# A GRU scan step: the scan's addends move from SBUF to PSUM, and the copy that feeds them moves from VectorE to ScalarE

## The chip, the core and the metric

The kernel runs on one core of a Trainium2 chip. The metric is device time in microseconds (us) of one execution. Engines are named as in the profile: PE (TensorE matmuls), PEld (TensorE weight loads), DVE (VectorE), ACT (ScalarE), POOL, SP. SBUF and PSUM are the core's two on-chip memories; matmuls write PSUM.

## The reference

Eight sequences of 256 steps with 256 channels go through a modulated linear layer and then a GRU, each with a residual:

```
ys = cond / 16;  d = rsqrt((ys*ys) @ (w*w) + 1e-8)
x  = x + ((x * ys) @ w) * d
for t in 0..255:
    Z = sigmoid(Xz[t] + H @ Whz.T + bhz)
    R = sigmoid(Xr[t] + H @ Whr.T + bhr)
    N = tanh(Xh[t] + (R*H) @ Whh.T + bhh)
    H = Z*H + (1 - Z)*N
    Y[t] = H @ Whq.T + bhq
x  = x + Y
```

Xz, Xr, Xh are x @ Wx.T + bx. The time goes into the 256 dependent steps.

## The kernel before

Channels lie on the 128 partitions in two chunks (k = 0, 1), so that one step's state is 2 x 8 columns. Time is cut into 16 blocks (n) of 16 steps (j). float32 is kept by splitting a factor into three bf16 parts; a product of weights and state is then six bf16 matmuls (3 x part 0, 2 x part 1, 1 x part 2), so that one gate of one step takes 24 small matmuls of 8 columns.

Each engine's program is written out by hand in its own order, and semaphores join them. One step t is:

- PE: 24 matmuls of gate R (they wait for `h_ready`, then `h_rest`, `h_rest2`), 12 of gate Z with 24 columns, one "bulk" matmul, 24 of gate G (these wait for `rh_ready`), five more bulk matmuls of 128 columns. Bulk is the work on other blocks, spread over the steps: for j < 4 the output Y of the block before, into `y_bank`, for j = 4 to 7 gate Z of the next block, into `z_bank`, for j >= 8 gates R and G of the next block, into `chunk_bank`. In 16 steps (n = 0 with j >= 4, n = 1 with j < 4) the bulk is one float32 matmul instead. Some steps have none (n = 0 with j < 4, n = 15 with j = 4 to 7).
- ACT: two sigmoids of R (L325, PSUM to PSUM), the sigmoid of -Z that writes 1 - Z into `scan_mul` (L327), two Tanh of the candidate N (L330), the copy that seeds gate Z's bank for the next step (L305), and in four steps of a block a copy that seeds a gate's bank (L311).
- DVE: R*H (L517) and its two remainders (L521, L525), a reduce that sums Z's partial products (L529), in most steps one 128-column instruction of the block work (L489 `finish`, L396 `take_z`, L413 `add_x`, L402, L409), two scans (L563), the remainders of the new H (L357, L361), and two copies (L364, L365).

The update of H is a scan over 24 columns, three for each sequence. It runs state = mul * state + add, with mul = 0, -1, 1-Z and add = h, N, h. That leaves h, then N - h, then (1-Z)(N-h) + h in the three columns, and the third is the new H. In `hidden[:, k, slot, 0:24]` the scan leaves its output; the addends lie in the same tensor, from column 2 of the slot before: h is in columns 2, 5, ... (the previous scan left it there), Tanh writes columns 3, 6, ..., and the copy L365 writes h once more to columns 4, 7, .... The scan waits for `g_ready`, which Tanh raises.

`r_gate` chooses the bank in which the R gate of a step lies: `r_bank` for k = 0, and for k = 1 `z_bank` while bulk works in `y_bank` (n > 0, j < 4), else `y_bank`.

Of the kernel before, what the change touches and what calls it, by code (L numbers as in the profile page):

```python
# [5 lines left out]
def modulated_linear_then_gru(  # L6
# [37 lines left out]
    ALU = mybir.AluOpType  # L44
    ACT = mybir.ActivationFunctionType

    P = 128
    KC = x_cm.shape[1]
    C = P * KC
    B = cond_cm.shape[2]  # L50
    T = x_cm.shape[2] // B
    BLOCK = 16
    BC = BLOCK * B
    SLOTS = 2 * BLOCK
# [11 lines left out]
    with ctx:  # L66
        def sb(name, shape, dt=fp32):
            return ctx.enter_context(nc.sbuf_tensor(name, shape, dt))
# [45 lines left out]


        PART = 3 * B
        hidden = sb("hidden", [P, KC, SLOTS, 2 * PART])
        hidden_parts = sb("hidden_parts", [P, KC, SLOTS, PARTS, B])
        r_hidden = sb("r_hidden", [P, KC, PARTS, B])
        z_pre = sb("z_pre", [P, KC, B])  # L120
# [14 lines left out]
        def h_scanned(k, slot):  # L135
            return hidden[:, k, slot, 2:PART:3]
# [19 lines left out]
        y_bank = pb("y_bank")  # L156
        r_bank = pb("r_bank")

        def r_gate(k, n, j):

            bank = r_bank if k == 0 else (z_bank if n > 0 and j < 4 else y_bank)
            return bank[:, KC * BC:KC * BC + B]

        def lin_bank(i, m):

# [2 lines left out]
        def pre(parity, gate, m, lo, hi):  # L168

            if gate == Z:  # L170
                return z_bank[:, m * BC + lo * B:m * BC + hi * B]
            at = 0 if gate == R else BC
            return chunk_bank[parity][m][:, at + lo * B:at + hi * B]
# [112 lines left out]
        @block.scalar  # L286
        def _(act):
            act.dma_start(cond[:, :, :], cond_cm).then_inc(ld_cond, 16)
            act.dma_start(w_mod[:, :, :], w_mod_cm).then_inc(ld_wmod, 16)
            act.dma_start(bias_rows[:, :, :], gate_bias[0:2, :, :]).then_inc(ld_bias, 16)  # L290
            act.dma_start(z_bx_bh[:, :, :], z_bias).then_inc(ld_zbias, 16)
            act.dma_start(bq[:, :], out_bias).then_inc(ld_bq, 16)

            act.wait_ge(ones_ready, 1)
            nc.scalar.activation(table_warm[:, :], ones[:, :], ACT.Sigmoid)
            act.wait_ge(ld_wrec, 16)
            for gate in GATE_ORDER:
                nc.scalar.activation(w_part[0][:, gate, :, :], w_rec[:, gate, :, :], ACT.Copy).then_inc(part_ready, 1)
            for i, gate in enumerate(GATE_ORDER):
                act.wait_ge(rest_ready, i + 1)  # L300
                nc.scalar.activation(w_part[1][:, gate, :, :], w_rec_rest[:, gate, :, :], ACT.Copy).then_inc(part_ready, 1)

            def seed_z(parity, j):

                nc.scalar.activation(  # L305
                    z_rec_bank[:, 0:KC * Z_GROUPS * B].rearrange("p (m g b) -> p m g b", m=KC, g=Z_GROUPS)[:, :, PARTS, :],
                    z_in[:, parity, :, j, :], ACT.Copy).then_inc(z_seeded, 1)

            def seed_gate(parity, gate, k):

                nc.scalar.activation(chunk_bank[parity][k][:, gate * BC:(gate + 1) * BC], bias_wide[:, k, gate, :],  # L311
                                     ACT.Copy).then_inc(gates_seeded, 1)

            act.wait_ge(wide_ready, 1)
            act.wait_ge(lin_ready, 1)
            for i in range(2 * KC):
                seed_gate(0, i // KC, i % KC)
            act.wait_ge(z_seeded, 1)
            act.wait_ge(lin_ready, 3)

            for t in range(T):
                p, j, n = t // BLOCK % 2, t % BLOCK, t // BLOCK
                for k in range(KC):
                    act.wait_ge(pre_r[k], t + 1)
                    nc.scalar.activation(r_gate(k, n, j), pre(p, R, k, j, j + 1), ACT.Sigmoid).then_inc(r_ready[k], 1)  # L325
                act.wait_ge(pre_z, t + 1)
                nc.scalar.activation(scan_mul[:, :, 2::3], z_pre[:, :, :], ACT.Sigmoid, scale=-1.0)  # L327
                for k in range(KC):
                    act.wait_ge(pre_g[k], t + 1)
                    nc.scalar.activation(hidden[:, k, (t - 1) % SLOTS, 3:3 + PART:3], pre(p, G, k, j, j + 1),  # L330
                                         ACT.Tanh).then_inc(g_ready[k], 1)
                if t + 1 < T:
                    seed_z((t + 1) // BLOCK % 2, (t + 1) % BLOCK)
                if n + 1 < NB and j in (4, 5, 6, 7):
                    if j == 4:
                        act.wait_ge(lin_ready, GROUPS)
                    seed_gate(1 - p, (j - 4) // KC, j % KC)

        @block.vector
        def _(dve):  # L340
# [8 lines left out]
            def split_h(slot, t1):  # L349
# [12 lines left out]
                                            ).then_inc(h_rest2[k], 1)  # L362
                if t1 <= T:
                    nc.vector.tensor_copy(h_word(every_chunk, slot), h_scanned(every_chunk, slot)).then_inc(h_packed, 1)  # L364
                nc.vector.tensor_copy(hidden[:, :, slot, 4:4 + PART:3], h_scanned(every_chunk, slot))  # L365

            nc.vector.memset(zeros[:, :], 0.0).then_inc(zeros_ready, 1)
            dve.wait_ge(ld_cond, 16)
# [135 lines left out]
            for t in range(T):  # L504
# [9 lines left out]
                    weight_split(6 + j % 2, 1 + (j - 4) // 2)  # L514
                for k in range(KC):
                    dve.wait_ge(r_ready[k], t + 1)
                    nc.vector.tensor_tensor(r_hidden[:, k, 0, :], r_gate(k, n, j), h_scanned(k, before),  # L517
                                            ALU.mult).then_inc(rh_ready[k], 1)
                for k in range(KC):
                    dve.wait_ge(rh_ready[k], t + 1)  # L520
# [2 lines left out]
                for k in range(KC):  # L523
# [6 lines left out]
                    z_pre[:, :, :], z_rec_bank[:, 0:KC * Z_GROUPS * B].rearrange(  # L530
                        "p (m g b) -> p m b g", m=KC, g=Z_GROUPS),
                    axis=mybir.AxisListType.X, op=ALU.add).then_inc(pre_z, 1)
                if n > 0 and j in (4, 5):
                    finish(n - 1, j - 4)
                if n + 1 < NB and j in (8, 9):
                    if j == 8:
                        dve.wait_ge(z_ready, n + 1)
                    take_z(1 - p, j - 8)
                if n == LAST and j in (14, 15):
                    finish_last(0, j - 14)  # L540
                if n == 0 and j < 4:
# [4 lines left out]
                    if j == 3:  # L546
                        mul.then_inc(lin_ready, 1)
                if NB // GROUPS <= n + 2 < NB:
                    if j == 10:
                        dve.wait_ge(lin_ready, GROUPS)  # L550
                    if j in (10, 11):
                        add_x(j - 10, slice((n + 2) * BC, (n + 3) * BC)).then_inc(x1_ready, 1)
                if n + 2 < NB:
                    if j in (12, 13):
                        if j == 12:
                            dve.wait_ge(x1_ready, x1_count(n + 2))
                        first_x1_rest(n + 2, j - 12)
                    if j in (14, 15):
                        second_x1_rest(n + 2, j - 14)

                for k in range(KC):
                    dve.wait_ge(g_ready[k], t + 1)
                    nc.vector.tensor_tensor_scan(hidden[:, k, t % SLOTS, 0:PART], scan_mul[:, k, :],  # L563
                                                 hidden[:, k, before, 2:2 + PART], 0.0, ALU.mult, ALU.add
                                                 ).then_inc(h_ready[k], 1)
                split_h(t % SLOTS, t + 2)

# [259 lines left out]
```

## Time and profile before

| | us |
|---|---|
| median of three runs | 640.48 (639.31 to 640.96) |
| the profiled execution | 639.56 |
| its span in the profile | 637.8 |
| lowest to highest of the three, share | 0.26% |

Busy shares of the span are 98% for PE, 89% for PEld, 77% for DVE and 33% for ACT. A busy share says little here: matmuls are pipelined and their ends are modelled, so that PE is shown as busy while the next matmul waits for its input. What a step waits for is read from the timeline of a step: where an instruction starts a few hundredths of a microsecond after another engine's instruction ended, that one released it.

### The profile page before, as it was taken

To read this page: it belongs to the slowest core of one execution; us is meant where nothing else is said; L and a number is where in the kernel's file an instruction comes from. 1 tells how busy PE (TensorE), PEld (TensorE's weight loads), DVE (VectorE), ACT (ScalarE), POOL (GpSimd) and SP (SyncE) were. 2 spreads that over 40 slices of the span, in tenths; PEclk is the share of its full clock that TensorE was granted. 3 is DMA by queue.
4 is the path that set the end of the run, shared out by engine and by line. 5 is a ranking of instruction groups with operands and counts; after the bars stand their busy time and mean duration, and the time that the engine had idled before them with its cause. 6 is when DMAs were issued, how large, how long until landed. Compare 5 with 4: busy or idle time off the path is not lost.

```text
span 637.8 us, 39807 instructions
## 1 busy us (share of the span) xinstructions
PE 626.3 (98%) x16890; PEld 568.1 (89%) x16890; DVE 491.6 (77%) x4051; ACT 209.1 (33%) x1607; POOL 4.5 (1%) x11
## 2 busy tenths in 40 slices
PE   8999999999999999999999999999999999999987
PEld 3689999999999999999999999999999999999976
DVE  5789777777877778777877877777777777877776
ACT  3133333333233333333333333333333333333332
POOL 2000000000000000000000000000000000000000
PEclk9955555555555555555555555555555555555555
DMA  7000000000000000000000000000000000000000
GB/s 264 2 5 3 4 13 4 13 4 12 4 5 12 5 12 4 12 5 4 13 4 13 4 5 12 5 12 5 12 5 4 12 4 13 4 13 4 4 12 12
DMA packets 7174, 8.86 MB, mean 14 GB/s; under 512 B 1618, under 2 KB 5458, under 8 KB 6996
## 3 DMA queue, kind: packets, MB, share of 16 engines
q1 hardware_dynamic: 6416, 6.03, 2.9%
q8 instruction: 133, 2.18, 1.4%
q14 instruction: 45, 0.37, 0.2%
q10 hardware_dynamic: 580, 0.28, 0.2%
HBM read 4.21 MB, written 2.10 MB: 10 GB/s over the span
## 4 chain that ended last, share of the span: by engine, by line
PE 93%; DVE 4%; ACT 1%; DMA 1%; issue 1%; DVEq 0%
PE chunk_bank L670 53%; PE z_rec_bank L670 13%; PE chunk_bank L647 12%; PE y_bank L632 6%; PE z_bank L647 6%; PE chunk_bank L679 1%; DMA x<-x_cm 1%; PE chunk_bank L584 1%; DVE lin L383 1%; DVE r_hidden L517 1%; DVE hidden L563 1%; DVE r_hidden L521 0%; DVE r_hidden L525 0%; ACT scan_mul L327 0%; DVE xs L376 0%
## 5 line engine op out<-in xcount | busy, mean ns | idle before, releaser
L670 PE MATMUL chunk_bank<-r_hidden,w_part 128*128 128x8 bf16 x6144 | 206.2, 169 | 0.2
L670 PEld LDWEIGHTS chunk_bank<-r_hidden,w_part 128*128 128x128 bf16 x6144 | 184.7, 105 | 17.9 <-issue 0.6
L670 PEld LDWEIGHTS chunk_bank<-hidden,w_part 128*128 128x128 bf16 x3072 | 102.5, 104 | 34.5 <-DVE hidden L563 6.2
L670 PE MATMUL chunk_bank<-hidden,w_part 128*128 128x8 bf16 x3072 | 125.1, 173 | 4.5 <-DVE hidden L563 4.0
L563 DVE TENSOR_TENSOR_SCAN hidden<-scan_mul,hidden 128x24 f32<-128x24 f32 x512 | 80.7, 199 | 60.0 <-ACT hidden L330 53.8
L327 ACT ACTIVATE scan_mul<-z_pre 128x16 f32<-128x16 f32 x256 | 57.2, 223 | 197.1 <-DVE z_pre L529 197.1
L670 PE MATMUL z_rec_bank<-hidden_parts,w_part 128*128 128x24 bf16 x3072 | 121.5, 181 | 0.1
L670 PE MATMUL chunk_bank<-hidden_parts,w_part 128*128 128x8 bf16 x3072 | 119.3, 168 | 0.0
L325 ACT ACTIVATE r_bank<-chunk_bank 128x8 f32<-128x8 f32 x256 | 41.5, 162 | 212.1 <-PE chunk_bank L670 206.6
L670 PEld LDWEIGHTS z_rec_bank<-hidden_parts,w_part 128*128 128x128 bf16 x3072 | 103.2, 104 | 0.2 <-DVE z_rec_bank L465 0.2
L670 PEld LDWEIGHTS chunk_bank<-hidden_parts,w_part 128*128 128x128 bf16 x3072 | 102.9, 104 | 0.0
L517 DVE TENSOR_TENSOR r_hidden<-r_bank,hidden 128x8 f32<-128x8 f32 x256 | 42.7, 167 | 73.4 <-ACT r_bank L325 73.2
L330 ACT ACTIVATE hidden<-chunk_bank 128x8 f32<-128x8 f32 x512 | 72.3, 179 | 3.1 <-PE chunk_bank L670 3.1
L357 DVE TENSOR_TENSOR hidden_parts<-hidden 128x8 f32<-128x8 f32 x514 | 71.3, 170 | 0.0
L361 DVE TENSOR_TENSOR hidden_parts<-hidden_parts 128x8 f32<-128x8 f32 x514 | 70.5, 167 | 0.0
L525 DVE TENSOR_TENSOR r_hidden<-r_hidden 128x8 f32<-128x8 f32 x512 | 70.3, 167 | 0.0
L521 DVE TENSOR_TENSOR r_hidden<-r_hidden 128x8 f32<-128x8 f32 x512 | 70.2, 167 | 0.0
L647 PE MATMUL chunk_bank<-x_rest,w_in 128*128 128x128 bf16 x224 | 58.4, 308 | 0.0
L529 DVE TENSOR_REDUCE z_pre<-z_rec_bank 128x16 f32<-128x64 f32 x256 | 55.7, 217 | 0.0
L305 ACT ACTIVATE z_rec_bank<-z_in 128x16 f32<-128x16 f32 x255 | 47.2, 185 | 0.0
L365 DVE COPY hidden<-hidden 128x16 f32<-128x16 f32 x257 | 44.5, 173 | 0.0
L632 PE MATMUL y_bank<-hidden_parts,w_out 128*128 128x128 bf16 x168 | 44.2, 295 | 0.0
(86 smaller groups left out, 667.3 us busy)
## 6 DMA issues: line engine op xcount, KB each, us to landing
x<-x_cm SPq DMA_DIRECT2D x4, 512.0 KB, 7.9
out_cm<-result SPq DMA_DIRECT2D x15, 128.0 KB, 2.1
w_rec<-w_rec_cm SPq DMA_DIRECT2D x1, 768.0 KB, 8.2
w_in<-w_in_cm SPq DMA_DIRECT2D x1, 768.0 KB, 9.8
w_mod<-w_mod_cm ACTq DMA_DIRECT2D x1, 256.0 KB, 5.7
w_out<-w_out_cm SPq DMA_DIRECT2D x1, 256.0 KB, 10.3
out_cm<-result SPq DMA_DIRECT2D x1, 64.0 KB, 2.9
out_cm<-result SPq DMA_DIRECT2D x2, 32.0 KB, 1.9
```

Source lines behind the costliest of these rows:

```text
L327: nc.scalar.activation(scan_mul[:, :, 2::3], z_pre[:, :, :], ACT.Sigmoid, scale=-1.0)
L330: nc.scalar.activation(hidden[:, k, (t - 1) % SLOTS, 3:3 + PART:3], pre(p, G, k, j, j + 1), ACT.Tanh).then_inc(g_ready[k], 1)
L357: nc.vector.tensor_tensor(h_word(k, slot, 1), h_scanned(k, slot), h_scanned_high(k, slot), ALU.subtract).then_inc(h_rest[k], 1)
L361: nc.vector.tensor_tensor(h_word(k, slot, 2), h_word(k, slot, 1), h_parts(k, slot, 1, 2), ALU.subtract).then_inc(h_rest2[k], 1)
L517: nc.vector.tensor_tensor(r_hidden[:, k, 0, :], r_gate(k, n, j), h_scanned(k, before), ALU.mult).then_inc(rh_ready[k], 1)
L521: nc.vector.tensor_tensor(r_hidden[:, k, 1, :], r_hidden[:, k, 0, :], rh_parts(k, 0, 1), ALU.subtract).then_inc(rh_rest[k], 1)
L525: nc.vector.tensor_tensor(r_hidden[:, k, 2, :], r_hidden[:, k, 1, :], rh_parts(k, 1, 2), ALU.subtract).then_inc(rh_rest2[k], 1)
L529: nc.vector.tensor_reduce(z_pre[:, :, :], z_rec_bank[:, 0:KC * Z_GROUPS * B].rearrange("p (m g b) -> p m b g", m=KC, g=Z_GROUPS), axis=myb ...
L563: nc.vector.tensor_tensor_scan(hidden[:, k, t % SLOTS, 0:PART], scan_mul[:, k, :], hidden[:, k, before, 2:2 + PART], 0.0, ALU.mult, ALU.ad ...
L632: mm = nc.tensor.matmul(y_bank[:, m * BC:(m + 1) * BC], W_OUT[wp][:, k, cols], h_parts(k, slice((1 - p) * BLOCK, (2 - p) * BLOCK), part, p ...
L647: mm = nc.tensor.matmul(pre(1 - p, gate, m, 0, BLOCK), W_IN[wp][:, gate, k, cols], x1_part(n + 1, k, part), start=(j == 4 and i == 0), sto ...
L670: return nc.tensor.matmul(cols, w_part[wp][:, gate, k, m * P:(m + 1) * P], moving, start=first, stop=True, skip_group_check=True)
```

## The change

Tanh now writes PSUM, into a stretch of 24 columns behind the R gate in the same bank, and the scan reads its 24 addends there. The two h columns of each three, which were there already (column 2) or were written by DVE (L365), are now both written by two ACT copies, `feed_scan`, one for each chunk. They wait for `h_ready` and stand behind the copy that seeds gate Z. DVE's copy L365 is gone, and `hidden` has half its width. The bank for k = 1 is chosen by `step_bank` so that bulk never works in it during the step; it is `z_bank` also for j = 8 and 9; `finish`, which reads `y_bank`, moves from j = 4, 5 to j = 8, 9, `take_z` from 8, 9 to 12, 13, `add_x` from 10, 11 to 4, 5, the first remainder of x from 12, 13 to 10, 11. Two waits are new on ACT, at the places where the copies for the next step would enter a bank in which bulk still works.

```diff
-        hidden = sb("hidden", [P, KC, SLOTS, 2 * PART])
+        hidden = sb("hidden", [P, KC, SLOTS, PART])
...
-        def r_gate(k, n, j):
-
-            bank = r_bank if k == 0 else (z_bank if n > 0 and j < 4 else y_bank)
-            return bank[:, KC * BC:KC * BC + B]
+        def step_bank(k, t):
+
+            n, j = t // BLOCK, t % BLOCK
+            return r_bank if k == 0 else (z_bank if n > 0 and (j < 4 or j in (8, 9)) else y_bank)
+
+        def r_gate(k, t):
+
+            return step_bank(k, t)[:, KC * BC:KC * BC + B]
+
+        def scan_add(k, t):
+
+            return step_bank(k, t)[:, KC * BC + 2 * B:KC * BC + 2 * B + PART]
...
+            def feed_scan(t):
+
+                for k in range(KC):
+                    act.wait_ge(h_ready[k], t + 1)
+                    nc.scalar.activation(scan_add(k, t).rearrange("p (b i) -> p b i", i=3)[:, :, 0::2],
+                                         h_scanned(k, (t - 1) % SLOTS).unsqueeze(2).to_broadcast([P, B, 2]), ACT.Copy)
...
-                    nc.scalar.activation(hidden[:, k, (t - 1) % SLOTS, 3:3 + PART:3], pre(p, G, k, j, j + 1),
+                    nc.scalar.activation(scan_add(k, t)[:, 1::3], pre(p, G, k, j, j + 1),
                                          ACT.Tanh).then_inc(g_ready[k], 1)
...
+                if t + 1 < T:
+                    if n > 0 and j == 3:
+                        act.wait_ge(y_ready, n)
+                    if 0 < n < NB - 1 and j == 7:
+                        act.wait_ge(z_ready, n + 1)
+                    feed_scan(t + 1)
...
-                nc.vector.tensor_copy(hidden[:, :, slot, 4:4 + PART:3], h_scanned(every_chunk, slot))
...
-                if n > 0 and j in (4, 5):
-                    finish(n - 1, j - 4)
+                if n > 0 and j in (8, 9):
+                    finish(n - 1, j - 8)
...
                     nc.vector.tensor_tensor_scan(hidden[:, k, t % SLOTS, 0:PART], scan_mul[:, k, :],
-                                                 hidden[:, k, before, 2:2 + PART], 0.0, ALU.mult, ALU.add
+                                                 scan_add(k, t), 0.0, ALU.mult, ALU.add
                                                  ).then_inc(h_ready[k], 1)
```

On ACT, an ordinary step in the middle of a block, from the sigmoid of Z to the next R sigmoids, stood before as

```order
L327 ACTIVATE scan_mul<-z_pre 128x16 [waits pre_z]
L330 ACTIVATE hidden<-chunk_bank 128x8 [waits pre_g0]
L330 ACTIVATE hidden<-chunk_bank 128x8 [waits pre_g1]
L305 ACTIVATE z_rec_bank<-z_in 128x2x8
L325 ACTIVATE r_bank<-chunk_bank 128x8 [waits pre_r0]
L325 ACTIVATE y_bank<-chunk_bank 128x8 [waits pre_r1]
```

and now stands, at the end of step j = 3, where the wait for bulk's last matmul in `y_bank` is added, as

```order
L343 ACTIVATE scan_mul<-z_pre 128x16 [waits pre_z]
L346 ACTIVATE r_bank<-chunk_bank 128x8 [waits pre_g0]
L346 ACTIVATE z_bank<-chunk_bank 128x8 [waits pre_g1]
L313 ACTIVATE z_rec_bank<-z_in 128x2x8
L326 ACTIVATE r_bank<-hidden 128x8x2 [waits h_ready0,y_ready]
L326 ACTIVATE y_bank<-hidden 128x8x2 [waits h_ready1]
L341 ACTIVATE r_bank<-chunk_bank 128x8 [waits pre_r0]
L341 ACTIVATE y_bank<-chunk_bank 128x8 [waits pre_r1]
```

Tanh's destination changed, and the two copies L326 came between the seed of gate Z and the R sigmoids of the next step.

On DVE, the end of step j = 4 of a block and the start of the next, with the block work in front of the scans, stood before as

```order
L529 TENSOR_REDUCE z_pre<-z_rec_bank 128x16 [waits rec_z]
L489 SCALAR_TENSOR_TENSOR result<-y_bank,bq,x 128x128 [waits stored1,y_ready]
L563 SCALAR_TENSOR_TENSOR hidden<-scan_mul,hidden 128x24 [waits g_ready0]
L563 SCALAR_TENSOR_TENSOR hidden<-scan_mul,hidden 128x24 [waits g_ready1]
L357 TENSOR_TENSOR hidden_parts<-hidden 128x8 [waits h_ready0]
L357 TENSOR_TENSOR hidden_parts<-hidden 128x8 [waits h_ready1]
L361 TENSOR_TENSOR hidden_parts<-hidden_parts 128x8 [waits h_rest0]
L361 TENSOR_TENSOR hidden_parts<-hidden_parts 128x8 [waits h_rest1]
L364 COPY hidden_parts<-hidden 128x2x8
L365 COPY hidden<-hidden 128x2x8
L517 TENSOR_TENSOR r_hidden<-r_bank,hidden 128x8 [waits r_ready0]
```

and the place where `finish` stands now, step j = 8, reads

```order
L550 TENSOR_REDUCE z_pre<-z_rec_bank 128x16 [waits rec_z]
L510 SCALAR_TENSOR_TENSOR result<-y_bank,bq,x 128x128 [waits stored1,y_ready]
L584 SCALAR_TENSOR_TENSOR hidden<-scan_mul,r_bank 128x24 [waits g_ready0]
L584 SCALAR_TENSOR_TENSOR hidden<-scan_mul,z_bank 128x24 [waits g_ready1]
L379 TENSOR_TENSOR hidden_parts<-hidden 128x8 [waits h_ready0]
L379 TENSOR_TENSOR hidden_parts<-hidden 128x8 [waits h_ready1]
L383 TENSOR_TENSOR hidden_parts<-hidden_parts 128x8 [waits h_rest0]
L383 TENSOR_TENSOR hidden_parts<-hidden_parts 128x8 [waits h_rest1]
L386 COPY hidden_parts<-hidden 128x2x8
L538 TENSOR_TENSOR r_hidden<-r_bank,hidden 128x8 [waits r_ready0]
```

The scans (shown as SCALAR_TENSOR_TENSOR) now have a PSUM bank as their second input, and the copy behind L364 is gone. PE's order is unchanged.

## Rows read from the trace of the kernel before

**Rows 1.** The page: granted clock of 40 slices, and the final chain by engine.
```profile
PEclk9955555555555555555555555555555555555555
...
PE 93%; DVE 4%; ACT 1%; DMA 1%; issue 1%; DVEq 0%
```

**Rows 2.** Three stretches of four steps: busy us (count) by engine, clock, DMA.
```profile
308.52:318.01 9.49, 9.49 (x267) 8.75 (x266) 7.53 (x63) 3.39 (x28) 0.00 (x0) 0.50 0.02 4
607.31:616.79 9.48, 7.99 (x246) 7.38 (x246) 7.06 (x62) 2.99 (x26) 0.00 (x0) 0.50 0.07 18
56.86:66.49 9.63, 9.57 (x249) 8.91 (x249) 8.38 (x67) 3.00 (x26) 0.00 (x0) 0.50 0.02 4
```

**Rows 3.** Timeline of one step's end: start, us, engine, line, instruction, count [idle before].
```profile
308.19 0.22 ACT L327 ACTIVATE scan_mul<-z_pre 128x16 f32<-128x16 f32 x1 [0.77 <-DVE z_pre L529]
...
308.31 0.29 ACT L330 ACTIVATE hidden<-chunk_bank 128x8 f32<-128x8 f32 x2
...
308.51 0.31 PE L647 MATMUL z_bank<-x_rest,w_in_rest 128*128 128x128 bf16 x1
...
308.52 0.32 DVE L563 TENSOR_TENSOR_SCAN hidden<-scan_mul,hidden 128x24 f32<-128x24 f32 x2 [0.36 <-ACT hidden L330]
...
308.59 0.27 ACT L311 ACTIVATE chunk_bank<-bias_wide 128x128 f32<-128x128 f32 x1
308.62 0.31 PE L647 MATMUL z_bank<-x_rest,w_in 128*128 128x128 bf16 x1
...
308.78 0.15 PEld L670 LDWEIGHTS chunk_bank<-hidden,w_part 128*128 128x128 bf16 x3
308.79 0.22 PE L670 MATMUL chunk_bank<-hidden,w_part 128*128 128x8 bf16 x2
```

**Rows 4.** The same timeline, a step without bulk.
```profile
607.57 0.49 PE L670 MATMUL chunk_bank<-hidden,w_part 128*128 128x8 bf16 x12 [0.41 <-DVE hidden L563]
```

**Rows 5.** ACT's instructions by line and shape: busy us, mean ns of one | idle before.
```profile
L330 ACT ACTIVATE hidden<-chunk_bank 128x8 f32<-128x8 f32 x512 | 72.3, 179 | 3.1 <-PE chunk_bank L670 3.1
L327 ACT ACTIVATE scan_mul<-z_pre 128x16 f32<-128x16 f32 x256 | 57.2, 223 | 197.1 <-DVE z_pre L529 197.1
L305 ACT ACTIVATE z_rec_bank<-z_in 128x16 f32<-128x16 f32 x255 | 47.2, 185 | 0.0
...
L325 ACT ACTIVATE y_bank<-chunk_bank 128x8 f32<-128x8 f32 x196 | 31.7, 162 | 0.0
```

**Rows 6.** DVE's instructions by line and shape.
```profile
L563 DVE TENSOR_TENSOR_SCAN hidden<-scan_mul,hidden 128x24 f32<-128x24 f32 x512 | 80.7, 199 | 60.0 <-ACT hidden L330 53.8
...
L521 DVE TENSOR_TENSOR r_hidden<-r_hidden 128x8 f32<-128x8 f32 x512 | 70.2, 167 | 0.0
...
L517 DVE TENSOR_TENSOR r_hidden<-y_bank,hidden 128x8 f32<-128x8 f32 x196 | 32.7, 167 | 0.0
...
L465 DVE TENSOR_SCALAR z_rec_bank<-z_bank,bias_z 128x8 f32<-128x8 f32 x2 | 0.4, 228 | 0.0
...
L440 DVE TENSOR_SCALAR d_sq<-z_rec_bank 128x16 f32<-128x16 f32 x1 | 0.2, 174 | 0.3 <-PE z_rec_bank L577 0.3
```

**Rows 7.** Timeline of DVE ahead of the steps.
```profile
18.81 1.28 DVE L383 TENSOR_TENSOR lin<-chunk_bank,d 128x512 f32<-128x512 f32 x2
20.01 1.28 DVE L376 TENSOR_TENSOR xs<-x,ys 128x512 f32<-128x512 f32 x2
```

**Rows 8.** Timeline of ACT, then of DVE, after the scans of Rows 3.
```profile
309.53 0.16 ACT L325 ACTIVATE r_bank<-chunk_bank 128x8 f32<-128x8 f32 x1 [0.66 <-PE chunk_bank L670]
...
309.24 0.17 DVE L365 COPY hidden<-hidden 128x16 f32<-128x16 f32 x1
309.72 0.17 DVE L517 TENSOR_TENSOR r_hidden<-r_bank,hidden 128x8 f32<-128x8 f32 x1 [0.30 <-ACT r_bank L325]
```

**Rows 9.** Timeline of DVE around a `finish`, step j = 4.
```profile
265.37 0.34 DVE L489 SCALAR_TENSOR_TENSOR result<-y_bank,bq,x 128x128 f32<-128x128 f32 x1
265.82 0.32 DVE L563 TENSOR_TENSOR_SCAN hidden<-scan_mul,hidden 128x24 f32<-128x24 f32 x2
```

More of the change, by code:

```diff
@@ L319, in _ @@
             act.wait_ge(lin_ready, 3)
+            feed_scan(0)
             for t in range(T):
@@ L324, in _ @@
                     act.wait_ge(pre_r[k], t + 1)
-                    nc.scalar.activation(r_gate(k, n, j), pre(p, R, k, j, j + 1), ACT.Sigmoid).then_inc(r_ready[k], 1)
+                    nc.scalar.activation(r_gate(k, t), pre(p, R, k, j, j + 1), ACT.Sigmoid).then_inc(r_ready[k], 1)
                 act.wait_ge(pre_z, t + 1)
@@ L516, in _ @@
                     dve.wait_ge(r_ready[k], t + 1)
-                    nc.vector.tensor_tensor(r_hidden[:, k, 0, :], r_gate(k, n, j), h_scanned(k, before),
+                    nc.vector.tensor_tensor(r_hidden[:, k, 0, :], r_gate(k, t), h_scanned(k, before),
                                             ALU.mult).then_inc(rh_ready[k], 1)
@@ L532, in _ @@
                     axis=mybir.AxisListType.X, op=ALU.add).then_inc(pre_z, 1)
-                if n > 0 and j in (4, 5):
-                    finish(n - 1, j - 4)
-                if n + 1 < NB and j in (8, 9):
-                    if j == 8:
+                if n > 0 and j in (8, 9):
+                    finish(n - 1, j - 8)
+                if n + 1 < NB and j in (12, 13):
+                    if j == 12:
                         dve.wait_ge(z_ready, n + 1)
-                    take_z(1 - p, j - 8)
+                    take_z(1 - p, j - 12)
                 if n == LAST and j in (14, 15):
@@ L548, in _ @@
                 if NB // GROUPS <= n + 2 < NB:
-                    if j == 10:
+                    if j == 4:
                         dve.wait_ge(lin_ready, GROUPS)
+                    if j in (4, 5):
+                        add_x(j - 4, slice((n + 2) * BC, (n + 3) * BC)).then_inc(x1_ready, 1)
+                if n + 2 < NB:
                     if j in (10, 11):
[L552 to L555, printed above, removed]
+                        if j == 10:
                             dve.wait_ge(x1_ready, x1_count(n + 2))
-                        first_x1_rest(n + 2, j - 12)
+                        first_x1_rest(n + 2, j - 10)
                     if j in (14, 15):
```

## The prediction

> **What bounds the kernel now.** I began with the page. PE's clock is granted in full for the first two slices and at half, 1.2 of 2.4 GHz, from there to the end, and the final chain lies on PE for 93% [rows 1]. That chain follows the modelled ends of matmuls and hides short waits between them, so I did not take it as proof that PE sets the pace. The second view is three stretches of four steps [rows 2]. The first is ordinary: 9.49 us, 2.37 us a step, 267 matmuls recorded. The second has no bulk at all, 246 matmuls, and takes 9.48 us. Twenty matmuls of 128 columns fewer changed nothing: bulk lies in the shade, and something else sets the step. The third stretch has one float32 matmul a step as bulk, and takes 9.63 us, 0.035 us a step more; only there does PE's own work last longer than what it covers.
>
> The third view, the end of one step [rows 3], shows what sets it. The first Tanh starts at 308.31, the first scan at 308.52, PE's weight load for the next step's gate R at 308.78, its first matmul at 308.79. So 0.21 us pass from Tanh to scan, about 0.18 of it Tanh and 0.03 the signal, and 0.26 us from scan to PE, about 0.20 of it scan and 0.06 the signal. Bulk's last two matmuls start at 308.51 and 308.62, 0.11 apart; a further one could have started at 308.73. R started at 308.79, so PE waited some 0.06 us for the scan. In the step without bulk the wait is open: 0.41 us idle, released by the scan [rows 4]. Hence the loop through h is the bound: R matmuls, sigmoid, R*H, G matmuls, Tanh, scan. What Tanh or the first scan gains or loses goes into each step one to one, as long as a gain stays under 0.06 us.
>
> **Tanh to PSUM.** Per step one Tanh (k = 0) lies on the loop; k = 1 runs 0.1 us behind it, like its scan. Tanh reads 8 columns of PSUM and writes SBUF: 179 ns mean. The sigmoid of gate R reads 8 columns of PSUM and writes 8 of PSUM: 162 ns [rows 5]. I take the difference, 17 ns. Bounds: what the trace does not show is a PSUM write with a stride of three words. If that costs as much as the SBUF write did, the gain is 0. At the other end, the sigmoid into `scan_mul` (16 columns, SBUF to SBUF, stride three) takes 223 ns and the seed of gate Z (16 columns, SBUF to PSUM, runs of eight) 185 [rows 5]; if all of that were the destination, the gain would be 38. 17 is the row with Tanh's own source and size.
>
> The Trainium skill bears on that stride: in "Advanced Engine Details and Errata", "PSUM Cachelines", it says that two neighbouring words should be contiguous, and that other patterns slow matmuls much. It speaks of matmuls, and no run here shows it for ScalarE; by it the gain of this part would go towards 0, 640.5 us.
>
> **The scan's addends from PSUM.** A scan takes 199 ns with both inputs in SBUF, and no row shows one with PSUM. The nearest rows are two-input instructions of 8 columns: R*H has one input in PSUM and takes 167 ns, its remainder has both in SBUF and takes 167 [rows 6]. With 512 columns, two in a row take 1.28 us from start to end with an input in PSUM (L383) and 1.28 without (L376), so neither the time of one nor the time until the next may start differs [rows 7]. Against it: L465 reads 8 columns of PSUM and takes 228 ns, 61 more. It has a per-partition operand, `bias_z`; L440 reads 16 columns of PSUM with a constant instead and takes 174 [rows 6]. I put the 61 on that operand, which the scan does not have. So I take 0, with -3 (a few ns of spread between such rows) and +61 as ends.
>
> The Trainium skill speaks against this part: "VectorE: DVE Perf Modes", "The TRN2 errata — SBUF-src ops pay a fixed extra latency per instruction", gives VectorE 58 cycles plus the columns from SBUF and 120 plus the columns from PSUM. That is an estimate of 65 ns a scan at its 0.96 GHz, and the time would be some 652 us. R*H and L383 do not agree with it, L465 does.
>
> **The copies of h, now on ACT.** 512 ACT copies are added, 2 a step, each with 16 columns from SBUF to PSUM like the seed of gate Z, 185 ns [rows 5]. They start when their scan is done, about 308.75 and 308.86. Queued behind them are the R sigmoids, for which PE and DVE wait; the first comes at 309.53, after 0.66 us in which ACT does nothing [rows 8]. The copies end at about 309.05: no cost, 0.45 us to spare. At j = 3 and j = 7 the first also waits for bulk's last matmul, which starts at 308.62 and ends at 308.93 [rows 3]; two copies from 308.97, the second 0.1 later, end by 309.3. The cover is 0.2 us there, in 29 steps. In the four steps of a block with a seed of a gate's bank the copies queue behind that as well: it ends at 308.86 [rows 3], and from there two copies end by 309.15. ACT's order also keeps Tanh behind the copies, so the scan needs no wait of its own for them.
>
> **DVE's copy goes.** L365 starts at 309.24 and holds DVE under 0.17 us, and R*H comes at 309.72 after 0.30 idle [rows 8]. What goes was in the shade: 0. In the 16 steps where a weight split stands between them, it can only help; 0 too.
>
> **The moved block work.** Each place has one 128-column instruction in front of the scans, before and after. `finish` takes 0.34 us and ends at 265.71, 0.11 us before the scan [rows 9]. None of the others takes longer, so any of them has room wherever it stands; 17 ns of that room is used up. The stores that `finish` releases start four steps later, and their buffer is wanted a block later: 0.
>
> **The sum.** 256 steps less 16 with float32 bulk, where PE is late by itself, are 240; 240 x 17 ns = 4.1 us. (If the 16 gain as well, it is 0.3 more.) The profiled execution took 639.56 us and would take 635.5. It lies 0.9 us under the median of the three runs, 640.48, so against that I say 636.4.
>
> **Rivals.**
> 1. The scan is slower from PSUM (slower). Place: from the first scan's start to `h_ready`, in every step. Price: up to 61 ns; net of Tanh 44 ns in 240 steps and 28 in the 16 where PE hides some 16, together 11.0 us: 651.5. It decides from 25 ns, where the net loss is 8 ns x 240 = 1.9 us. For it speaks L465, against it R*H, L383 and L440.
> 2. Nothing is left (no change): the strided write costs what SBUF did, or a scan loses the 9 to 25 ns that cancel the gain. 640.5, give or take 1.9. For it: no row shows either form, and `scan_mul`, strided, is the slowest ACT row of its size.
> 3. PE is the bound, and scans that are ready earlier wait for it: 640.5. For it the 93% of the chain, against it the two equal stretches and the 0.41 us idle. Only the part beyond 60 ns could be lost so.
> 4. More is gained: Tanh 38 ns less, and 3 from the scan. 240 x 41 ns = 9.8 us, 630.6. For it the 38 ns between L327 and L305, against it that these differ in function and stride.
>
> **How the numbers follow.** A measurement of this kernel tells about 0.3% (1.9 us) from no change. I give the forecast, a net of 10 to 21 ns a step (638.1 to 635.4), 0.58; rival 1 0.13; rival 2 0.15; rival 3 0.04; rival 4 with all beyond 21 ns 0.10. Faster is the forecast and rival 4: 0.68. Same is rivals 2 and 3: 0.19. Slower is rival 1: 0.13. For the range I leave out rival 1 and the far end of rival 4 (beyond 28 ns, about 0.04): 633.7 to 642.0. The forecast's own range is 635.4 to 638.1.
>
> **What would show it.** Tanh's row near 162 ns and the scan's still near 199; four ordinary steps in 9.42 us instead of 9.49, with PE's first R matmul still 0.06 us behind the end of the first scan; four steps with float32 bulk still in 9.63; 512 more ACT copies of some 185 ns that end well before the R sigmoid; DVE's idle time before R*H longer than 0.30 us. I am wrong if the scan's row is longer by more than the Tanh's is shorter, if Tanh's row stays at 179, or if an R sigmoid starts right behind a copy of h.

## The result, and the profile after

| | before | after |
|---|---|---|
| median of 8 runs (lowest to highest) | 640.85 us (639.31 to 641.26) | 637.36 us (634.85 to 638.07) |
| profiled execution (span) | 639.56 us (637.8) | 637.65 us (635.9) |
| first scan to last scan, from the profiles | 605.4 us | 600.8 us |

The ratio is 0.9944, with an interval of 0.9929 to 0.9958: 0.56% faster, 3.5 us. The prediction was 4.1 us and 636.4.

The first view is three stretches of four steps in the kernel after: ordinary, without bulk, with float32 bulk. The columns are those of [rows 2].

```profile
309.35:318.76 9.41, 9.41 (x266) 8.69 (x265) 7.11 (x59) 4.46 (x36) 0.00 (x0) 0.50 0.07 18
...
605.71:615.13 9.42, 7.96 (x246) 7.33 (x246) 6.66 (x58) 4.16 (x34) 0.00 (x0) 0.50 0.02 4
...
59.58:69.21 9.63, 9.57 (x249) 8.97 (x249) 8.04 (x62) 4.16 (x34) 0.00 (x0) 0.50 0.01 3
```

The first two were 9.49 and 9.48, so a step without float32 bulk is now some 18 ns shorter. The third is 9.63 as before. ACT carries about 1 us more in each, and that costs nothing.

The timeline of one step's end, as in [rows 3] and [rows 8], shows the new order. ACT now has the two copies L326 between the seeds and the next sigmoid.

```profile
309.02 0.22 ACT L343 ACTIVATE scan_mul<-z_pre 128x16 f32<-128x16 f32 x1 [0.77 <-DVE z_pre L550]
...
309.15 0.17 ACT L346 ACTIVATE r_bank<-chunk_bank 128x8 f32<-128x8 f32 x1
...
309.25 0.16 ACT L346 ACTIVATE y_bank<-chunk_bank 128x8 f32<-128x8 f32 x1
...
309.35 0.20 DVE L584 TENSOR_TENSOR_SCAN hidden<-scan_mul,r_bank 128x24 f32<-128x24 f32 x1 [0.35 <-ACT r_bank L346]
...
309.47 0.18 DVE L584 TENSOR_TENSOR_SCAN hidden<-scan_mul,y_bank 128x24 f32<-128x24 f32 x1
...
309.61 0.49 PE L691 MATMUL chunk_bank<-hidden,w_part 128*128 128x8 bf16 x12
309.63 0.18 ACT L326 ACTIVATE r_bank<-hidden 128x16 f32<-128x16 f32 x1
...
309.73 0.17 ACT L326 ACTIVATE y_bank<-hidden 128x16 f32<-128x16 f32 x1
...
310.34 0.16 ACT L341 ACTIVATE r_bank<-chunk_bank 128x8 f32<-128x8 f32 x1 [0.43 <-PE chunk_bank L691]
...
310.54 0.17 DVE L538 TENSOR_TENSOR r_hidden<-r_bank,hidden 128x8 f32<-128x8 f32 x1 [0.40 <-ACT r_bank L341]
```

PE's first matmul of R still starts 0.06 us behind the end of the first scan (309.55). The copies end at 309.90 and the sigmoid comes at 310.34. DVE's idle time before R*H went from 0.30 to 0.40.

By line and shape, as in [rows 5], ACT's Tanh now has a row for each chunk k (and one more for `z_bank`, where k = 1 writes in the other steps). It took 179 ns before.

```profile
L343 ACT ACTIVATE scan_mul<-z_pre 128x16 f32<-128x16 f32 x256 | 57.2, 224 | 196.8 <-DVE z_pre L550 196.8
...
L346 ACT ACTIVATE r_bank<-chunk_bank 128x8 f32<-128x8 f32 x256 | 42.9, 168 | 3.0 <-PE chunk_bank L691 3.0
...
L346 ACT ACTIVATE y_bank<-chunk_bank 128x8 f32<-128x8 f32 x166 | 26.9, 162 | 0.0
```

And DVE's scans, against 199 ns in [rows 6]:

```profile
L584 DVE TENSOR_TENSOR_SCAN hidden<-scan_mul,r_bank 128x24 f32<-128x24 f32 x256 | 52.0, 203 | 58.0 <-ACT r_bank L346 52.2
...
L584 DVE TENSOR_TENSOR_SCAN hidden<-scan_mul,y_bank 128x24 f32<-128x24 f32 x166 | 29.6, 178 | 0.0
```

The 199 was a mean over two kinds. Taken apart by the starts and ends of the trace (steps 32 to 239, where no float32 bulk is), the first scan of a step took 207.6 ns before and 203.3 after, the second 190.3 and 178.6; the first Tanh 175.9 and 167.7, the second 183.1 and 162.0. From the same starts and ends I cut a step along its chain, for both kernels and five of the experiments below. "R's last" is the 20th of gate R's 24 matmuls, the last that the sigmoid of chunk 0 needs (it waits for `h_rest2` of chunk 1).

| mean ns | before | after | e_tanh | e_scan | e_tanh_k0 | e_tanh_k1 | e_zpsum |
|---|---|---|---|---|---|---|---|
| first scan's start to R's first matmul | 264.6 | 260.5 | 265.7 | 262.0 | 266.6 | 265.9 | 261.9 |
| to R's last | 528.0 | 528.5 | 527.2 | 526.1 | 529.2 | 529.8 | 527.0 |
| to the sigmoid's start | 209.8 | 204.2 | 204.4 | 209.8 | 212.4 | 204.2 | 210.8 |
| sigmoid, R*H, to G's first matmul | 417.3 | 417.4 | 417.6 | 418.9 | 417.6 | 418.0 | 418.4 |
| G's first matmul to the first Tanh | 742.9 | 741.6 | 742.1 | 740.9 | 742.7 | 741.8 | 735.0 |
| first Tanh | 175.9 | 167.7 | 167.5 | 176.9 | 167.0 | 176.4 | 162.0 |
| to the next first scan | 32.9 | 32.2 | 31.5 | 32.0 | 31.2 | 31.9 | 32.1 |
| second scan's end behind R's first matmul (not in the sum) | 50.6 | 38.8 | 41.7 | 48.9 | 54.6 | 41.0 | 49.5 |
| R's 20th to its 21st matmul (not in the sum) | 32.2 | 26.7 | 26.9 | 32.3 | 34.9 | 26.7 | 33.3 |
| a step | 2371.4 | 2352.1 | 2356.3 | 2366.7 | 2366.7 | 2368.1 | 2347.2 |

A step lost 19.3 ns: 8.2 in the first Tanh, 5.6 between R's last matmul and its sigmoid, 4.1 from scan to PE, and 1.3 on the way to Tanh. Over 239 steps that is 4.6 us, which is what the table at the top has from first to last scan. Yet the profiled executions differ by 1.9 us only. The rest is lost before the first step. Here is the first row of the linear layer on PE, before and then after (the same timeline, 0 to 14 us):

```profile
7.53 3.67 PE L679 MATMUL chunk_bank<-xs,w_mod 128*128 128x512 f32 x8 [1.89 <-DVE xs L376]
```

```profile
7.51 6.51 PE L700 MATMUL chunk_bank<-xs,w_mod 128*128 128x512 f32 x8 [1.88 <-DVE xs L397]
```

The same eight matmuls, after the same idle time, take 2.84 us longer, and the first scan starts at 31.0 us instead of 28.2. The change does not touch this code. So 4.6 us were gained in the steps and 2.8 lost at the start in this execution; the two "warm" runs below ask whether that is chance.

### The profile page after: what moved, and what is told of

Same layout as the page of the kernel before. It is cut to its first block, busy times and chain, and to the rows that moved or that the text cites. A ratio compares the mean times of both kernels' runs of the same rounds, so it can differ in the third digit from the quotient of the medians.

```text
span 635.9 us, 40091 instructions
## 1 busy us (share of the span) xinstructions
PE 624.7 (98%) x16890; PEld 566.6 (89%) x16890; DVE 465.4 (73%) x3794; ACT 279.5 (44%) x2119; POOL 4.5 (1%) x11
## 3 DMA queue, kind: packets, MB, share of 16 engines
q8 instruction: 133, 2.18, 1.4%
## 4 chain that ended last, share of the span: by engine, by line
PE 93%; DVE 4%; ACT 1%; DMA 1%; issue 1%; DVEq 0%
PE chunk_bank L691 53%; PE z_rec_bank L691 13%; PE chunk_bank L668 12%; PE z_bank L668 6%; PE y_bank L653 6%; PE chunk_bank L700 2%; DMA x<-x_cm 1%; PE chunk_bank L605 1%; DVE lin L404 1%; DVE r_hidden L538 1%; DVE hidden L584 1%; DVE r_hidden L542 0%; DVE r_hidden L546 0%; ACT scan_mul L343 0%; DVE xs L397 0%
## 5 line engine op out<-in xcount | busy, mean ns | idle before, releaser
L691 PE MATMUL chunk_bank<-hidden_parts,w_part 128*128 128x8 bf16 x3072 | 117.8, 168 | 0.0
L691 PEld LDWEIGHTS chunk_bank<-hidden_parts,w_part 128*128 128x128 bf16 x3072 | 101.5, 104 | 0.0
L584 DVE TENSOR_TENSOR_SCAN hidden<-scan_mul,r_bank 128x24 f32<-128x24 f32 x256 | 52.0, 203 | 58.0 <-ACT r_bank L346 52.2
L341 ACT ACTIVATE r_bank<-chunk_bank 128x8 f32<-128x8 f32 x256 | 41.4, 162 | 111.4 <-PE chunk_bank L691 111.4
L379 DVE TENSOR_TENSOR hidden_parts<-hidden 128x8 f32<-128x8 f32 x514 | 68.3, 170 | 0.0
L383 DVE TENSOR_TENSOR hidden_parts<-hidden_parts 128x8 f32<-128x8 f32 x514 | 67.5, 167 | 0.0
L326 ACT ACTIVATE r_bank<-hidden 128x16 f32<-128x16 f32 x256 | 47.6, 186 | 25.9 <-DVE z_rec_bank L486 5.5
L346 ACT ACTIVATE r_bank<-chunk_bank 128x8 f32<-128x8 f32 x256 | 42.9, 168 | 3.0 <-PE chunk_bank L691 3.0
```

The costliest lines, as they stand in the source:

```text
L326: nc.scalar.activation(scan_add(k, t).rearrange("p (b i) -> p b i", i=3)[:, :, 0::2], h_scanned(k, (t - 1) % SLOTS).unsqueeze(2).to_broadc ...
L379: nc.vector.tensor_tensor(h_word(k, slot, 1), h_scanned(k, slot), h_scanned_high(k, slot), ALU.subtract).then_inc(h_rest[k], 1)
L383: nc.vector.tensor_tensor(h_word(k, slot, 2), h_word(k, slot, 1), h_parts(k, slot, 1, 2), ALU.subtract).then_inc(h_rest2[k], 1)
L691: return nc.tensor.matmul(cols, w_part[wp][:, gate, k, m * P:(m + 1) * P], moving, start=first, stop=True, skip_group_check=True)
```

## Experiments

**e_tanh: Tanh to PSUM alone.** The kernel after, whose scan reads its addends from a constant tile in SBUF.

```diff
+        add_sb = sb("add_sb", [P, KC, PART])
...
-                                                 scan_add(k, t), 0.0, ALU.mult, ALU.add
+                                                 add_sb[:, k, :], 0.0, ALU.mult, ALU.add
```

> The changed kernel, but the scan reads its addends from a constant SBUF tensor, so that the candidate N and h do not enter the new state; Tanh still writes PSUM and ScalarE's copies still run. Measured is the time from the first to the last scan of the 256 steps: 605.4 us before, 600.8 us with the change, in the 239 or so steps without float32 bulk 2371 ns before and 2352 after, so 19 ns to explain. My theory: 10 of them are Tanh's (its k = 0 row fell from 176 to 168 ns, and 2 ns fell in front of it), 4 are the first scan's own row (207 to 203 ns), and 6 come from the second scan (190 to 178 ns, and its start 5 ns nearer the first), because its remainders no longer hold up the last matmuls of gate R. Then this kernel takes 603.0 us from first to last scan (2361 ns a step), with Tanh's rows as with the change and the scans' as before. Rival 1, all of it is Tanh's, and the scans are shorter only because Tanh's end came earlier: 600.8 us. Rival 2, it is VectorE's copy that went (this kernel has none either): 600.8 us too, and the kernel before less its copy would show it.

Measured: 637.42 us (median of 7; before on the same chip 641.35, ratio 0.9936, 0.9913 to 0.9959). The profile's source view of the scan gives its durations (least, median, greatest) and its first and last start:

```profile
L586 DVE TENSOR_TENSOR_SCAN hidden<-scan_mul,add_sb x512: 180/196/209, 29.7 to 631.4; 128x24 f32<-128x24 f32 x171
```

From first to last scan 601.75 us, 3.6 less than before; 15.1 ns a step.

**e_scan: the scan's addends from PSUM alone.** Tanh writes an SBUF tile that nobody reads, and the copies fill all three columns of the addends.

```diff
...
-                    nc.scalar.activation(scan_add(k, t)[:, 1::3], pre(p, G, k, j, j + 1),
+                    nc.scalar.activation(tanh_sb[:, k, 1::3], pre(p, G, k, j, j + 1),
```

> The changed kernel, but Tanh writes an SBUF tensor that nothing reads, with the stride it had before, and ScalarE's copies of h fill all three columns of the scan's addends in PSUM, so that h stands where the candidate N should. The scan still reads PSUM. My theory: Tanh's rows are as before (176 and 183 ns), the scans' as with the change (203 and 178 ns), a step takes 2361 ns, and the first scan is 603.1 us ahead of the last. Rival 1 (all is Tanh's): 605.4 us, scans at 207 and 190 ns. Rival 2 (VectorE's copy that went): 600.8 us.

Measured: 639.95 us (median of 10, ratio 0.9979, 0.9963 to 0.9995), 604.19 from first to last scan, 4.7 ns a step gained. The scans by source:

```profile
L585 DVE TENSOR_TENSOR_SCAN hidden<-scan_mul,r_bank x256: 203/204/206, 28.0 to 632.0; 128x24 f32<-128x24 f32 x128
...
L585 DVE TENSOR_TENSOR_SCAN hidden<-scan_mul,y_bank x166: 183/190/194, 28.1 to 632.1; 128x24 f32<-128x24 f32 x166
```

The first scan's row is 204 ns with its addends in PSUM, and 208 with them in SBUF (before and e_tanh). That is a small gain where the forecast had none and rival 1 a loss. The two parts add up within what one profile tells of a step (see b_warm and e_warm): 15.1 and 4.7 are 19.8, and the whole change gave 19.3. I had expected them to share it about evenly; Tanh has three quarters.

**e_nocopy_moves: VectorE's copy gone and the block work moved, nothing else.** The kernel before without L365 (the third addend of each sequence is then a constant zero), with `finish`, `take_z`, `add_x` and `first_x1_rest` where the change has them.

```diff
-                nc.vector.tensor_copy(hidden[:, :, slot, 4:4 + PART:3], h_scanned(every_chunk, slot))
...
-                if n > 0 and j in (4, 5):
-                    finish(n - 1, j - 4)
+                if n > 0 and j in (8, 9):
+                    finish(n - 1, j - 8)
```

> The kernel before, with VectorE's copy of h (L365) left out, so that the third addend is a constant zero, and with finish, take_z, add_x and the first remainder of x moved to the steps where the change has them. Tanh and scan stay in SBUF. My theory: both edits lie in the shade, the first scan is 605.4 us ahead of the last (2371 ns a step). Rival 2 (the copy held up what follows, VectorE or SBUF): 2352 to 2365 ns a step, 600.8 to 603.9 us. It clears the state tensor once before the steps, which may cost up to 3 us ahead of the first scan and is not counted.

Measured: 639.69 us in one run, 605.7 us from first to last scan, 2372.9 ns a step against 2371.4. The two edits gain nothing, as forecast.

**e_feed6: four more copies of h a step on ACT**, behind the two that feed the scan. If there is 0.45 us to spare, they fit.

```diff
+                    for i in range(4):
+                        nc.scalar.activation(
+                            r_bank[:, 2 * B * i:2 * B * (i + 1)].rearrange("p (b i) -> p b i", i=2),
+                            h_scanned(i % KC, t % SLOTS).unsqueeze(2).to_broadcast([P, B, 2]), ACT.Copy)
```

> The changed kernel with four more ScalarE copies of h in each step, behind the two, into columns of r_bank that nothing reads. My theory: ScalarE has about 0.45 us to spare between the copies and the next R sigmoid, a copy holds it for about 0.1 us, so six of them end just before the sigmoid and the step stays at 2352 ns, 600.8 us from first to last scan. Rival: the copies are not free, because they read the state while TensorE and VectorE read it, or because the sigmoid comes late behind them: then four more cost at least twice what the two did, and each 4 ns a step more is 1 us.

Measured: 636.92 us in one run; 2361.5 ns a step, 9.4 more than after. ACT's timeline in an ordinary step, and then at the end of step j = 7, where the copies wait for bulk's last matmul:

```profile
317.33 0.48 ACT L361 ACTIVATE r_bank<-hidden 128x16 f32<-128x16 f32 x4
317.86 0.16 ACT L341 ACTIVATE r_bank<-chunk_bank 128x8 f32<-128x8 f32 x1
```

```profile
310.42 0.48 ACT L361 ACTIVATE r_bank<-hidden 128x16 f32<-128x16 f32 x4
310.85 0.12 ACT L341 ACTIVATE r_bank<-chunk_bank 128x8 f32<-128x8 f32 x1
```

In the ordinary step six copies end at 317.81 and the sigmoid starts 0.05 us later. At j = 7 the sigmoid starts right behind them, with no idle time, and so it does at j = 3. From that step's first scan to the next it takes 2412 ns there instead of 2352, which is four fifths of the whole loss; the other steps take 2352 to 2359, 2354 in the mean. So six copies fit too, with nothing left over, except where they start late. The 0.45 us that I had read as spare was nearly right: with two copies ACT is idle for 0.46 us in a step without a seed of a gate's bank, for 0.43 in a step with one, and for 0.25 where they wait for bulk. What I got wrong is that I left those last steps out.

**e_tanh_k0 and e_tanh_k1: one chunk's Tanh to PSUM at a time.** e_tanh gave 15.1 ns, but the first Tanh's row only 8.4; 5.4 came between R's last matmul and its sigmoid. New theory: the second chunk is on the loop as well. Its Tanh, its scan and the bfloat16 remainders made from it feed R's last matmuls, and before the change those came some 6 ns late. Rival: only the first chunk counts, as the prediction has it. Both kernels are e_tanh with one Tanh left in SBUF (the cut is k0; k1 has `k == 1`).

```diff
...
-                    nc.scalar.activation(scan_add(k, t)[:, 1::3], pre(p, G, k, j, j + 1),
+                    nc.scalar.activation((scan_add(k, t) if k == 0 else tanh_sb[:, k, :])[:, 1::3], pre(p, G, k, j, j + 1),
```

> The kernel of e_tanh (the scan reads constant addends from SBUF, so N and h do not enter the state), with only the first chunk's Tanh (k = 0) writing PSUM and the second's an SBUF tensor that nothing reads, as before. The runs so far say that Tanh for both chunks takes 15 ns off a step (2371 to 2356), and that the second scan ends 240 ns after its own Tanh, whatever its row says. My new theory: gate R needs both chunks, the first chunk's h for its start and the second's remainders for its last matmuls, and before the change the second chunk was late by some 6 ns. Then the first chunk alone gives next to nothing: its 11 ns turn into a longer wait at gate R's end, with the sigmoid some 217 ns or more behind the last matmul's start instead of 210, and a step takes 2366 to 2371 ns. Rival (only the first chunk is on the loop, as I predicted): 2356 to 2361 ns, with 210 ns or less.

> The same with only the second chunk's Tanh (k = 1) writing PSUM. New theory: the second chunk is no longer late, the 6 ns at gate R's end go (204 ns from the last matmul's start to the sigmoid's), the first chunk sets the loop with its old Tanh row of 176 ns, and a step takes 2365 ns. Together the two single gains (0 to 5, and 6) come to less than the 15 of both. Rival (only the first chunk counts): 2371 ns.

Measured, one run each beside 639.85 of before: 640.08 with k = 0 alone and 640.57 with k = 1 alone; 4.7 and 3.3 ns a step gained. The Tanh rows by shape, of k0 and then of k1:

```profile
L348 ACT ACTIVATE tanh_sb<-chunk_bank 128x8 f32<-128x8 f32 x256 | 46.3, 181 | 0.0
L348 ACT ACTIVATE r_bank<-chunk_bank 128x8 f32<-128x8 f32 x256 | 42.8, 167 | 3.0 <-PE chunk_bank L694 3.0
```

```profile
L348 ACT ACTIVATE tanh_sb<-chunk_bank 128x8 f32<-128x8 f32 x256 | 45.1, 176 | 3.0 <-PE chunk_bank L694 3.0
...
L348 ACT ACTIVATE y_bank<-chunk_bank 128x8 f32<-128x8 f32 x166 | 26.9, 162 | 0.0
```

The rival is out. With k = 0 alone the first Tanh gains its 9 ns, but the time from R's last matmul to the sigmoid grows to 212.4, since the second scan now ends 54.6 ns behind R's first matmul instead of 50.6. With k = 1 alone it ends after 41.0, that time falls to 204.2, and the first Tanh keeps its 176. The table shows the join over all seven kernels: where the second scan ends 39 to 42 ns behind R's first matmul, R's sigmoid comes 204 ns after the last matmul's recorded start; at 49 to 51 it is 210 to 211, at 55 it is 212. The wait itself stands in the table one record later. R's 20th matmul waits for the second chunk's second remainder, and the 21st starts 32 to 35 ns behind it in before, e_scan, e_tanh_k0 and e_zpsum, but 26.7 to 26.9 in after, e_tanh and e_tanh_k1, the same 26.7 as between the matmuls in front. Each alone gives less than both together, 4.7 and 3.3 of the 15 ns. The step of e_tanh_k1, 2368, lies between the 2365 of the theory and the 2371 of the rival and does not decide by itself; the wait that is gone does. The few ns that the singles lose besides are spread over the matmul terms of the table, and what makes them is open.

**b_warm and e_warm: the start.** Before the linear layer PE multiplies ten tiles of zeros, and then idles some 1.9 us until `xs` is there. Here it is fifteen, in the kernel before and in the one after.

```diff
-            for _ in range(10):
+            for _ in range(15):
```

> The kernel before with 15 instead of 10 matmuls of zeros on TensorE at the start. The profiles so far differ ahead of the steps: the first eight float32 matmuls of the linear layer took 3.67 us before and 6.51 with the change, and the first scan came at 28.2 and 31.0 us. My theory: this is when TensorE's clock rises from half to full, which falls early or late by chance in any kernel, and hides part of the gain in single runs. With five more matmuls TensorE is busy without a gap until the linear layer's input is there at 7.5 us, the clock should be full by then in every run, so the first scan comes at 28.2 us or a little later and the median falls by 0.5 to 1.5 us, to about 639.5 to 640.5. Rival: the time of the rise does not depend on this stretch; then the median stays where it is or rises by the 0.2 us by which the five end too late.

> The changed kernel with 15 instead of 10 matmuls of zeros. My theory: 634.9 us (the 639.56 us of the profiled run before, which had an early rise, less the 4.6 us that the steps lost), and against the kernel before with the same 15 matmuls a difference of 4.6 us. Rival (the change itself slows the start): 637.4 us, with the first scan at about 31 us again.

Measured: b_warm 639.75 us (12 runs, 639.54 to 640.22; ratio to before 0.998, 0.997 to 0.9989), e_warm 635.20 (5 runs, 635.16 to 635.38; ratio 0.9906, 0.9891 to 0.9921). PE's first rows in e_warm:

```profile
1.19 5.28 PE L708 MATMUL y_bank<-zeros 128*128 128x512 bf16 x15 [1.19 <-DVE zeros L388]
7.17 3.67 PE L700 MATMUL chunk_bank<-xs,w_mod 128*128 128x512 f32 x8 [0.71 <-DVE xs L397]
```

In e_warm the idle time is 0.71 us, the eight matmuls take the short 3.67 us, and the first scan starts at 27.9 us (in b_warm no idle time, 3.66 and 28.0). The spread of the runs shrinks from 2 us and more to 0.7 and 0.2. With ten tiles the first scan came at 28.0 to 28.2 in before, e_scan, e_nocopy_moves and e_feed6, and at 29.7 to 31.0 in after, e_tanh, e_tanh_k0, e_tanh_k1 and e_zpsum: kernels of both kinds, in code that none of them changes. I take it as chance of the execution.

These rows put the lost time on TensorE's clock. In the trace of before the eight matmuls start 0.43 us apart (the first two 0.50); in after they start 0.85 us apart (the first two 0.98) until 12.8 us, and the last follows after 0.67. In e_tanh_k0, e_tanh_k1 and e_zpsum the trace has the granted clock of this stretch, and it is at the lower of its two levels (1.2 of 2.4 GHz) just where the starts are 0.85 us apart: in e_tanh_k0 from 7.2 to 10.7 us, after 2.85 us of idle time, and for part of the stretch in the other two, after 2.17 and 2.18. The means from 7.5 to 11.0 us are 0.55, 0.72 and 0.63 there, against 1.00 in before. Here is that stretch in before and in e_tanh_k0; the first count is that of the matmuls, and the clock is the third number from the end:

```profile
7.50:11.00 3.50, 3.48 (x8) 1.62 (x9) 2.29 (x4) 0.66 (x2) 0.00 (x0) 1.00 1.06 415
```

```profile
7.50:11.00 3.50, 3.35 (x5) 1.57 (x6) 2.41 (x5) 0.62 (x2) 0.00 (x0) 0.55 1.03 403
```

For after the view shows 1.00 too, but its trace has no record of the clock before 13.2 us, where it is full; that it was low before is read from the 0.85 us alone. Why it is low in one execution and not in another after the same 1.9 us of idle time is open.

With the late start gone, the change is worth 639.75 - 635.20 = 4.55 us, about the 4.6 of the steps. The two profiled executions differ by 5.0 us from first to last scan: a step of b_warm took 2375.0 ns, 3.6 more than one of before, and a step of e_warm 2354.1, 2.0 more than one of after, in the same step code. So a step read from one profile can be off by 2 to 4 ns (e_zpsum and e_zpsum_warm agree, 2347.2 in both), and a difference like e_scan's 4.7 or e_tanh_k1's 3.3 stands on its rows and terms more than on its step.

**e_zpsum and e_zpsum_warm: one step further.** The sigmoid of Z (`scan_mul`) reads `z_pre` from SBUF and takes 224 ns, and the first Tanh comes right behind it on ACT. If it reads PSUM instead, it should be shorter.

```diff
-        z_pre = sb("z_pre", [P, KC, B])
...
+        z_pre = r_bank[:, 0:KC * B].rearrange("p (k b) -> p k b", k=KC)
```

> The changed kernel, with the sum of gate Z's partial products (z_pre) written by VectorE's reduce into free columns of r_bank instead of SBUF. The first Tanh starts 122 ns after the sigmoid of Z in every one of the steps, some 6 ns later than its own matmul allows, and its row is 168 ns where the second Tanh's is 162: I take it that the sigmoid holds ScalarE, for longer because its input is in SBUF. My theory: with its input in PSUM the sigmoid holds ScalarE under 110 ns, the first Tanh starts 4 to 6 ns earlier and takes 162 ns, a step takes 2342 ns and the first scan is 598.4 us ahead of the last. Rival 1: VectorE's reduce gets slower by writing PSUM and gives that back, 600.8 us. Rival 2: the first Tanh waits for its matmul alone, 600.8 us as well, but with the 122 ns shorter.

> Both: z_pre in PSUM, and 15 matmuls of zeros. If both theories hold, 632.5 us; if neither does, 637.4.

Measured: e_zpsum 635.20 us (6 runs, ratio 0.9895, 0.9877 to 0.9913), 599.58 from first to last scan. ACT, then DVE, by line and shape:

```profile
L344 ACT ACTIVATE scan_mul<-r_bank 128x16 f32<-128x16 f32 x256 | 49.2, 192 | 199.1 <-DVE r_bank L551 199.1
...
L347 ACT ACTIVATE r_bank<-chunk_bank 128x8 f32<-128x8 f32 x256 | 41.5, 162 | 3.0 <-PE chunk_bank L692 3.0
```

```profile
L551 DVE TENSOR_REDUCE r_bank<-z_rec_bank 128x16 f32<-128x64 f32 x256 | 57.7, 225 | 0.0
...
L585 DVE TENSOR_TENSOR_SCAN hidden<-scan_mul,y_bank 128x24 f32<-128x24 f32 x166 | 31.7, 191 | 0.0
```

The sigmoid fell to 192, the first Tanh to 162, and it starts 6.6 ns earlier behind G's first matmul than after (735.0 against 741.6). But 4.9 ns a step came out instead of some 10: the second chunk is late again (its scan ends 49.5 ns behind R's first matmul, R's 21st matmul comes 33.3 behind the 20th, and R's sigmoid at 210.8), the same join as in e_tanh_k0. With fifteen zero tiles, e_zpsum_warm takes 633.46 us (4 runs, 633.37 to 633.68; ratio 0.9879, 0.9862 to 0.9896). It is faster than both kernels, 1.2% below before.

## Why the prediction was right, point by point

**What bounds the kernel.** The loop through h, as said. Nineteen ns off the chain came out of each ordinary step and nothing out of the 16 with float32 bulk (2406.3 ns before, 2406.7 after; 9.63 us for four in both), where PE is late by itself. Rival 3 is out.

**Tanh to PSUM.** The size was right, 17 forecast and 15.1 measured alone, but the path was only half of it. I took 17 from the sigmoid's row and put it on the first chunk. The first Tanh gave 8.2, since before it was not a 179 ns instruction but one of 176, and after it lasts 168 and not 162, until e_zpsum shortens the `scan_mul` ahead of it. The other part came through the second chunk. The step that failed is "k = 1 runs 0.1 us behind it, like its scan": I read the second scan's start as a distance to the loop and did not follow k = 1 to the join at R's last matmuls, where it was some 6 ns late. The strided write to PSUM costs nothing extra on ScalarE: 162 ns is the sigmoid's row with contiguous words. Rivals 2 and 4 are out.

**The scan from PSUM.** Forecast 0, measured some 4 ns gained, just beyond the 3 that I had as the lower end: the first scan's mean row is 203 to 204 ns in all six kernels with addends in PSUM and 208 to 209 in all six with them in SBUF (the step of e_scan says 4.7). Rival 1 is out: L465's 61 ns are not the price of a PSUM source. I put them on its per-partition operand, but L465 also writes PSUM where L440 writes SBUF, and no run here takes the two apart. The Trainium skill's rule ("VectorE: DVE Perf Modes", "The TRN2 errata — SBUF-src ops pay a fixed extra latency per instruction"), 58 cycles plus the columns from SBUF against 120 from PSUM, is not what this scan shows: 203 ns from PSUM and 208 from SBUF. R*H [rows 6] had said so.

**The copies on ACT.** Free as forecast, and 0.43 us of idle time is left in a step with a seed. At j = 3, where they wait for bulk's last matmul, ACT's timeline has:

```profile
265.12 0.19 ACT L326 ACTIVATE r_bank<-hidden 128x16 f32<-128x16 f32 x1 [0.30 <-PE y_bank L653]
265.24 0.17 ACT L326 ACTIVATE y_bank<-hidden 128x16 f32<-128x16 f32 x1
...
265.66 0.16 ACT L341 ACTIVATE r_bank<-chunk_bank 128x8 f32<-128x8 f32 x1 [0.25 <-PE chunk_bank L691]
```

They end at 265.41 and 0.25 us are left; I had worked out 0.2.

**VectorE's copy and the block work.** Nothing, as forecast (e_nocopy_moves, 1.5 ns a step longer in one run).

**The sum.** 4.1 us was forecast, 4.6 came in the steps, and the medians show 3.5, as the start of the ten-tile kernel takes up to 2.8 us more or less by chance. Neither the forecast nor its range had a term for that, only the 1.9 us that a measurement can tell. The forecast's 17 ns a step and the 19.3 measured are made of different parts: the first Tanh gave half of what was forecast, and the join at R's last matmuls and the scan, both forecast at nothing, gave the rest. So the path through h and the sign were understood, and the closeness of the number is partly luck.

## What to carry to other kernels

In a loop that works in chunks, follow every chunk to where they meet: a later start is no slack, and a gain on one chunk alone is partly lost where it waits for the other. When an edit is worth less than the start of the program varies, compare from the first step to the last instead of whole times, or make the start steady first; and run a kernel's steps twice before reading a few ns from them. A mean over a line can mix two kinds of instruction, one that waits behind its predecessor and one that doesn't; take them apart before putting a difference on an operand.

## What the runs showed of the hardware

- The second scan ended 242 ns after the end of its own Tanh before (addends in SBUF) and 236 in after, e_scan and e_zpsum (PSUM), though its row is 179 ns in after and 190 in e_scan. It began 121 ns behind the first scan in both. A shorter row there meant that Tanh had ended earlier ahead of it, not a faster scan.
- An ACT instruction that reads 16 columns from PSUM instead of SBUF took 192 ns instead of 224, and a DVE reduction that writes 16 columns to PSUM instead of SBUF took 225 instead of 217.
- Eight float32 matmuls after 1.9 us of idle time took 3.67 us in one execution, with starts 0.43 us apart, and 6.51 in another, with starts 0.85 us apart for most of them. Where the granted clock of that stretch was recorded, it was at its lower level just where the starts were 0.85 us apart (e_tanh_k0, e_tanh_k1, e_zpsum). After 0.71 us of idle time they took 3.67 us, after none 3.66.
